# A graph convolution on one core: eight groups of every twenty routed on chip instead of seven, with a new order of work

## The chip, the cores and the metric

The kernel runs on one core of a Trainium2 chip. The metric is the device time in microseconds of one execution. The kernel before took 2231.55 us (median of three runs, 2224.62 to 2231.94).

## The reference

```
h   = x @ W_in2f                                     # 6250 nodes x 128
Wij = (ssp(f_ij @ W_filt1 + b_filt1) @ W_filt2 + b_filt2) * weight[:, None]   # 200000 edges
agg = segment_sum(h[dst] * Wij, src, 6250)           # a sum per node over its edges
out = ssp(agg @ W_out1 + b_out1) @ W_out2 + b_out2   # ssp(v) = softplus(v) - log 2
y   = layernorm(x + out)
```

The edges are sorted by `dst`, so the rows `h[dst]` of neighbouring edges lie close together. `src`, the index of the sum, is in random order. Everything is float32; `f_ij` has 20 columns.

## The kernel before

**Tiling.** 200000 edges are 391 groups of 512 (four tiles of 128). Twenty groups make a *unit*; there are 19 full units and a rest of eleven groups (380 to 390). A prologue forms `h`, splits it into three bf16 parts, writes it to HBM, and works out positions for the routed groups. An epilogue adds the partial sums and does the two output layers and the layer norm in 13 chunks.

**Every group** goes through the same front part. TensorE does the first filter layer for two groups at once (`first_layer`, L1773). ScalarE takes abs, exp and ln of it, VectorE finishes `hidden` (L1301). TensorE does the second layer (`second_layer`, a bias matmul at L1782 and the product at L1786). TensorE picks the rows `h[dst]` from a window of 128 rows with a one-hot (`gather`, L1811), ScalarE scales them by the edge weight (L874), and VectorE multiplies the two (`multiply`, L1327) into the message.

**How a message is summed** is one of two ways. A *plain* group builds an equality matrix `same` (VectorE L1280), TensorE sums repeated indices within a tile (`sum_repeated`, L1799), ScalarE copies the result out (`copy_total`, L857), VectorE makes the index (`mark_repeated` L1337, `make_index` L1346), and GpSimd issues four indirect DMAs, one for each tile, that add 128 rows of 512 B into one of four tables in HBM (`scatter`, L716). `total` has four buffers, and `copy_total` waits until the adds of the plain group that held its buffer have landed (`rows_landed`).

A *routed* group never leaves the chip. ScalarE and VectorE split its message into two float32r parts (`split_hi` L885, `split_lo` L1353). VectorE builds four one-hots of 128x896 (`route_one_hot`, L1365). TensorE multiplies them to sort the messages into seven slot tiles (`route`, four matmuls each, L1829). ScalarE keeps each in a ring of seven (`keep_slots`, L898). Then one slot tile for each of the seven newest groups gets a one-hot (`slot_one_hot`, L1382), TensorE sums the seven (`sum_slots`, 28 matmuls, L1848), and VectorE adds the two halves of the result to `acc_t` (`add_slice`, L1399). `route_hot` has one buffer and `unit_psum` two banks, used by `route` and `sum_slots` in turn: `route(m, 0)` and `route(m, 1)` wait for the two adds of the sums before them, and later ones wait for the ring copy two back.

**Order.** TensorE, ScalarE and VectorE each follow a list written out by hand for a unit (`unit(u)`), and another for the rest (`rest()`). GpSimd and SyncE go group by group. `m(n)` and `r(n)` count routed groups in the unit, `g(n)` groups, `pair(n)` pairs. `ROUTED_AT` says which groups of a unit are routed: seven of twenty, and three in the rest, 136 in all.

Of the kernel before, what the change touches and what calls it, by code (L numbers as in the profile page):

```python
# [60 lines left out]
META_HOTS, META_STEPS = 20, 49  # L61
# [15 lines left out]
assert BUCKETS * BUCKET == NODE_ROWS > NODES and RING == PER_UNIT == SLOT_TILES and UNIT % 4 == 0  # L77
# [200 lines left out]
def build(nc, t):  # L278
    with ExitStack() as ctx:
# [89 lines left out]
        local = at(39872, "local", [P, ROUTES * TILES], F32)  # L369
        src_r = at(42048, "src_r", [P, ROUTES * TILES], I32)  # L370
        rank = at(44224, "rank", [P, UNITS * PER_UNIT * TILES], F32)
        rank_part = at(46464, "rank_part", [P, ROUTES * TILES], F32)
        in_bucket = at(48640, "in_bucket", [P, BUCKETS, ROUTES * TILES], BF16)
        h_rest = at(63872, "h_rest", [P, 2, 4, DIM], F32)
        bias_tmp = at(67968, "bias_tmp", [P, 2, 3, DIM], F32)
        bias_hi = at(71040, "bias_hi", [P, 2, 3, DIM], BF16)
        base_all = at(72576, "base_all", [P, SLOTS], F32)
        spread_row = at(74208, "spread_row", [1, SLOTS], F32)
# [386 lines left out]
        def _(act):  # L765
# [135 lines left out]
            def unit(u):  # L901
                def g(n): return plus(u, n)
                def pair(n): return (u[0], u[1] // 2 + n)
                def m(n): return (u[0], u[1] // UNIT * PER_UNIT + n)
                def r(n): return (u[0], u[1] // UNIT * PER_UNIT + n)
                soften_ln(pair(2))
                keep_slots(m(0), 0)
                weigh_h_dst(g(3), plain)
                copy_total(g(0), plain)
                keep_slots(m(0), 1); keep_slots(m(0), 2)  # L910
                soften_abs(pair(3))
                keep_slots(m(0), 3); keep_slots(m(0), 4)
                soften_exp(pair(3))
                keep_slots(m(0), 5); keep_slots(m(0), 6)
                soften_ln(pair(3))
                weigh_h_dst(g(4), plain)
                split_hi(r(0))
                weigh_h_dst(g(5), plain)
                copy_total(g(1), plain)
                weigh_h_dst(g(6), plain)  # L920
                soften_abs(pair(4))
                keep_slots(m(1), 0)
                copy_total(g(3), plain)
                keep_slots(m(1), 1)
                soften_exp(pair(4))
                keep_slots(m(1), 2)
                soften_ln(pair(4))
                keep_slots(m(1), 3); keep_slots(m(1), 4); keep_slots(m(1), 5); keep_slots(m(1), 6)
                split_hi(r(1))
                columns(g(10), plain)  # L930
                soften_abs(pair(5))
                weigh_h_dst(g(7), plain)
                copy_total(g(4), plain)
                soften_exp(pair(5))
                weigh_h_dst(g(8), plain)
                soften_ln(pair(5))
                keep_slots(m(2), 0); keep_slots(m(2), 1); keep_slots(m(2), 2); keep_slots(m(2), 3)
                copy_total(g(6), plain)
                keep_slots(m(2), 4)
                weigh_h_dst(g(9), plain)  # L940
                keep_slots(m(2), 5)
                weigh_h_dst(g(10), plain)
                keep_slots(m(2), 6)
                split_hi(r(2))
                soften_abs(pair(6))
                soften_exp(pair(6))
                soften_ln(pair(6))
                copy_total(g(7), plain)
                keep_slots(m(3), 0)
                weigh_h_dst(g(11), plain)  # L950
                copy_total(g(9), plain)
                keep_slots(m(3), 1); keep_slots(m(3), 2); keep_slots(m(3), 3); keep_slots(m(3), 4)
                weigh_h_dst(g(12), plain)
                soften_abs(pair(7))
                keep_slots(m(3), 5); keep_slots(m(3), 6)
                soften_exp(pair(7))
                soften_ln(pair(7))
                weigh_h_dst(g(13), plain)
                split_hi(r(3))
                weigh_h_dst(g(14), plain)  # L960
                copy_total(g(10), plain)
                soften_abs(pair(8))
                keep_slots(m(4), 0)
                soften_exp(pair(8))
                weigh_h_dst(g(15), plain)
                keep_slots(m(4), 1); keep_slots(m(4), 2)
                soften_ln(pair(8))
                keep_slots(m(4), 3); keep_slots(m(4), 4); keep_slots(m(4), 5); keep_slots(m(4), 6)
                copy_total(g(12), plain)
                weigh_h_dst(g(16), plain)  # L970
                split_hi(r(4))
                soften_abs(pair(9))
                soften_exp(pair(9))
                weigh_h_dst(g(17), plain)
                keep_slots(m(5), 0)
                soften_ln(pair(9))
                copy_total(g(13), plain)
                keep_slots(m(5), 1); keep_slots(m(5), 2)
                columns(g(20), plain)
                weigh_h_dst(g(18), plain)  # L980
                keep_slots(m(5), 3); keep_slots(m(5), 4); keep_slots(m(5), 5)
                soften_abs(pair(10))
                keep_slots(m(5), 6)
                soften_exp(pair(10))
                soften_ln(pair(10))
                copy_total(g(15), plain)
                split_hi(r(5))
                weigh_h_dst(g(19), plain); weigh_h_dst(g(20), plain)
                soften_abs(pair(11))
                keep_slots(m(6), 0); keep_slots(m(6), 1)  # L990
                soften_exp(pair(11))
                keep_slots(m(6), 2); keep_slots(m(6), 3)
                soften_ln(pair(11))
                keep_slots(m(6), 4)
                weigh_h_dst(g(21), plain)
                keep_slots(m(6), 5); keep_slots(m(6), 6)
                copy_total(g(17), plain)
                split_hi(r(6))
                soften_abs(pair(12))
                weigh_h_dst(g(22), plain)  # L1000
                soften_exp(pair(12))
                copy_total(g(18), plain)

            def rest():
                weigh_h_dst((0, 383), plain)
                keep_slots((0, 133), 0)
                soften_ln((0, 192))
                keep_slots((0, 133), 1); keep_slots((0, 133), 2)
                copy_total((0, 380), plain)
                keep_slots((0, 133), 3)  # L1010
                soften_abs((0, 193))
                keep_slots((0, 133), 4); keep_slots((0, 133), 5); keep_slots((0, 133), 6)
                weigh_h_dst((0, 384), plain)
                soften_exp((0, 193))
                soften_ln((0, 193))
                copy_total((0, 381), plain)
                split_hi((0, 133))
                weigh_h_dst((0, 385), plain)
                soften_abs((0, 194))
                weigh_h_dst((0, 386), plain)  # L1020
                keep_slots((0, 134), 0)
                copy_total((0, 383), plain)
                keep_slots((0, 134), 1); keep_slots((0, 134), 2); keep_slots((0, 134), 3)
                keep_slots((0, 134), 4); keep_slots((0, 134), 5); keep_slots((0, 134), 6)
                split_hi((0, 134))
                soften_exp((0, 194))
                soften_ln((0, 194))
                weigh_h_dst((0, 387), plain)
                copy_total((0, 384), plain); copy_total((0, 386), plain)
                keep_slots((0, 135), 0); keep_slots((0, 135), 1); keep_slots((0, 135), 2)  # L1030
# [687 lines left out]
        def _(pe):  # L1718
# [135 lines left out]
            def unit(u):  # L1854
# [3 lines left out]
                def r(n): return (u[0], u[1] // UNIT * PER_UNIT + n)  # L1858
# [264 lines left out]
```

## Time and profile before

| | us |
|---|---|
| median of three runs | 2231.55 |
| lowest and highest run | 2224.62, 2231.94 |
| span of the profiled execution | 2225.5 |
| TensorE matmul busy, weight load busy | 2054.4 (92%), 1691.5 (76%) |
| VectorE busy | 1898.8 (85%) |
| ScalarE busy | 1594.9 (72%) |
| GpSimd busy | 1754.4 (79%) |

The profile gives no time of its own for the profiled execution besides its span, 2225.5 us; the three runs lie between 0.9 us below and 6.4 us above that. The busy shares are means over prologue, main part and epilogue. The main part is from about 105 to 2140 us.

### The profile page before, as it was taken

What the parts mean: (1) busy time and instruction counts of PE and PEld (TensorE: products, weight loads), DVE (VectorE), ACT (ScalarE), POOL (GpSimd) and SP (SyncE); (2) the same over time, 40 slices, a digit from 0 to 9 for tenths busy, and PEclk for the clock granted to TensorE, in tenths of its full rate; (3) what the DMA queues carried; (4) which work ended last, traced back from release to release, by engine and by line L of the source; (5) the groups of instructions that cost most, each with busy time, mean ns of one, the idle gap of its engine ahead of it and who ended that gap; (6) DMA issues with size and microseconds to landing.
All of it is one profiled execution on the core that took longest, in us unless ns stands there. A gap on an engine that the chain in (4) does not pass through costs nothing.

```text
span 2225.5 us, 54062 instructions
## 1 busy us (share of the span) xinstructions
PE 2054.4 (92%) x15953; PEld 1691.5 (76%) x15953; DVE 1898.8 (85%) x3919; ACT 1594.9 (72%) x3812; POOL 1754.4 (79%) x1078
## 2 busy tenths in 40 slices
PE   3589999999999999999999999999999999999946
PEld 2477878787887878887888788888878887877733
DVE  6578989898998988988999888988989988988837
ACT  0378777777777777877777777877777777877617
POOL 2058888888888888888888888888888888888874
PEclk9699999999999999999999999999999999999978
DMA  9556666665666565655666656656666665666495
GB/s 329 191 99 95 97 100 99 89 100 90 98 98 100 93 92 92 107 96 87 102 97 96 97 90 97 98 92 96 96 101 97 95 99 92 93 100 94 52 223 141
DMA packets 353785, 239.34 MB, mean 108 GB/s; under 512 B 86919, under 2 KB 332786, under 8 KB 353338
## 3 DMA queue, kind: packets, MB, share of 16 engines
q0 software_dynamic: 146736, 66.85, 32.2%
q1 hardware_dynamic: 196326, 152.61, 27.4%
q10 hardware_dynamic: 10476, 16.77, 2.0%
q8 instruction: 133, 2.18, 0.4%
q14 instruction: 114, 0.93, 0.1%
HBM read 147.25 MB, written 88.83 MB: 106 GB/s over the span
## 4 chain that ended last, share of the span: by engine, by line
DMA 33%; PE 30%; POOL 14%; issue 13%; DVE 5%; ACT 4%; POOLq 0%; ACTq 0%; DVEq 0%; SPq 0%
DMA table<-total,index 31%; POOL table L716 14%; PE unit_psum L1829 7%; PE unit_psum L1848 6%; PE both_psum L1786 6%; PE total_psum L1799 4%; PE pre_psum L1773 3%; PE both_psum L1811 2%; PE both_psum L1782 2%; DMA h_parts<-h_out 1%; ACT out_rows L1087 1%; ACT total L857 1%; DMA b_o<-in_b_o 1%; DVE scat_hot L1382 1%; DVE route_hot L1365 0%
## 5 line engine op out<-in xcount | busy, mean ns | idle before, releaser
L716 POOL DMA_INDIRECT table<-total,index x1019 | 1695.7, 1664 | 419.6 <-issue 252.5
L1829 PE MATMUL unit_psum<-moving,route_hot 128*128 128x258 f32 x3808 | 604.7, 298 | 5.5 <-ACT ring L898 3.2
L1829 PEld LDWEIGHTS unit_psum<-moving,route_hot 128*128 128x128 f32 x3808 | 497.9, 192 | 68.6 <-ACT ring L898 49.9
L898 ACT ACTIVATE ring<-unit_psum 128x258 fp32r<-128x258 f32 x952 | 354.1, 394 | 242.6 <-PE unit_psum L1829 225.5
L874 ACT ACTIVATE h_dst<-both_psum,cols 128x128 f32<-128x128 f32 x1564 | 446.3, 374 | 95.3 <-PE both_psum L1811 92.5
L1848 PE MATMUL unit_psum<-scat_hot,ring 64*128 64x448 f32 x3808 | 462.2, 380 | 8.1 <-DVE acc_t L1399 4.2
L1382 DVE TENSOR_SCALAR scat_hot<-node_iota,ring 128x448 fp32r<-128x448 uint16 x952 | 434.7, 476 | 6.8 <-ACT ring L898 4.7
L1786 PEld LDWEIGHTS both_psum<-w_f,hidden 128*128 128x128 f32 x3128 | 426.1, 197 | 11.8
L1786 PE MATMUL both_psum<-w_f,hidden 128*128 128x128 f32 x3128 | 423.9, 279 | 0.0
L1365 DVE TENSOR_SCALAR route_hot<-node_iota,cols 128x896 fp32r<-128x896 uint16 x544 | 378.4, 713 | 43.7 <-PE unit_psum L1829 42.9
L1848 PEld LDWEIGHTS unit_psum<-scat_hot,ring 64*128 64x128 f32 x3808 | 340.2, 186 | 87.5 <-ACT ring L898 30.3
L1799 PE MATMUL total_psum<-message,same 128*128 128x129 f32 x2040 | 284.7, 283 | 33.9 <-ACT total L857 33.1
L1799 PEld LDWEIGHTS total_psum<-message,same 128*128 128x128 f32 x2040 | 258.2, 197 | 56.8 <-issue 54.2
L1301 DVE SCALAR_TENSOR_TENSOR hidden<-pre_psum,soft 128x1024 f32<-128x1024 f32 x196 | 238.3, 1216 | 45.3 <-ACT soft L850 45.2
L857 ACT ACTIVATE total<-total_psum 128x516 f32<-128x516 f32 x255 | 154.7, 607 | 119.8 <-DMA table<-total,index 110.1
L1773 PE MATMUL pre_psum<-f_t,w_f 32*128 32x512 f32 x784 | 222.8, 644 | 7.0 <-issue 4.3
L838 ACT ACTIVATE soft<-pre_psum 128x1024 f32<-128x1024 f32 x196 | 201.8, 1030 | 30.4 <-PE pre_psum L1773 30.1
L1327 DVE TENSOR_TENSOR message<-both_psum,h_dst 128x512 f32<-128x512 f32 x255 | 174.2, 683 | 43.6 <-PE both_psum L1786 40.7
L844 ACT ACTIVATE soft<-soft 128x1024 f32<-128x1024 f32 x196 | 209.7, 1070 | 1.3
L850 ACT ACTIVATE soft<-soft 128x1024 f32<-128x1024 f32 x196 | 208.8, 1065 | 2.0
L1399 DVE TENSOR_TENSOR acc_t<-acc_t,unit_psum 128x448 f32<-128x448 f32 x284 | 166.8, 611 | 11.4 <-PE unit_psum L1848 10.8
L1811 PE MATMUL both_psum<-window,pick 128*128 128x128 bf16 x1564 | 158.1, 225 | 16.6 <-DVE pick L1291 10.0
(118 smaller groups left out, 1517.7 us busy)
## 6 DMA issues: line engine op xcount, KB each, us to landing
dst_b<-dst SPq DMA_DIRECT2D x391, 128.0 KB
src_b<-src SPq DMA_DIRECT2D x255, 128.0 KB
f_t<-in_f_t SPq DMA_DIRECT2D x100, 256.0 KB, 3.7
table<-total,index POOLq DMA_INDIRECT x1019
table<-zeros ACTq DMA_DIRECT2D x20, 640.0 KB, 10.1
window<-h_parts SPq DMA_DIRECT2D x391, 32.0 KB
parts<-table SPq DMA_DIRECT2D x48, 256.0 KB, 5.4
h_parts<-h_out SPq DMA_DIRECT2D x12, 384.0 KB, 2.9
```

Source lines behind the costliest of these rows:

```text
L716: pool.indirect_dma_start(tables[table], bass.IndirectOffsetOnAxis(index[:, i, k:k + 1], 0), total[:, i, k, 0:DIM], None, compute_op=ALU.a ...
L844: act.activation(soft[:, :, :], soft[:, :, :], ACT.Exp, scale=-1.0).then_inc(exp_done, 1)
L874: last = act.activation(h_dst[:, b, d], source, ACT.Copy, scale=cols[:, g[1] // HALF % 2, weight:weight + 1])
L898: act.activation(ring[:, r[1] % RING, k, :], unit_psum[:, k % 2, 0:MOVING], ACT.Copy).then_inc(ring_done, 1)
L1301: dve.scalar_tensor_tensor(hidden[:, first:first + 2, :], pre_psum[:, :, :], 0.0, soft[:, :, :], ALU.max, ALU.add).then_inc(hidden_done, 1)
L1365: hot = dve.tensor_scalar(route_hot[:, tile, :], node_iota[:, :], cols[:, half, column:column + 1], None, ALU.is_equal)
L1382: dve.tensor_scalar(scat_hot[:, r[1] % RING, :], node_iota[:, 0:BUCKET], ring[:, r[1] % RING, k, 2 * DIM:2 * DIM + 1].bitcast(F32), None, ...
L1773: last = pe.matmul(pre_psum[:, a, :], w_f1[row:row + BAND, :], f_t[row:row + BAND, quad[1] % FEEDS, :], start=True, stop=True)
L1786: last = pe.matmul(filter_psum[:, d], hidden[:, g[1] % QUAD, k * P:(k + 1) * P], w_f2[:, :], start=False, stop=(k == TILES - 1))
L1799: last = pe.matmul(total_psum[:, k // 2, d], same[:, b, k, :], message[:, b, k, :], start=True, stop=True)
L1829: last = pe.matmul(unit_psum[:, k % 2, 0:MOVING], route_hot[:, tile, k * P:(k + 1) * P], moving[:, tile, :], start=(tile == 0), stop=(tile ...
L1848: last = pe.matmul(unit_psum[:, strip, 0:BUCKET], ring[rows, r[1] % RING, slot_tile(m), part * DIM:(part + 1) * DIM], scat_hot[rows, r[1] ...
```

## The change

`ROUTED_AT` gets an eighth group in every unit, and the rest a fourth: 156 routed groups and 235 plain ones instead of 136 and 255. The arrays for the routed groups' positions grow with them (624 columns instead of 544). A memset in the prologue goes, and a wait for the column copy is written out ahead of the one-hots. The order lists of TensorE, ScalarE and VectorE are written anew, for the unit and for the rest; the ring of seven and the sums over seven groups stay.

```diff
-ROUTED_AT = (2, 5, 8, 11, 14, 16, 19)
-LAST_ROUTED = (382, 385, 387)
+ROUTED_AT = (1, 3, 6, 8, 11, 13, 16, 18)
+LAST_ROUTED = (381, 383, 386, 388)
 PER_UNIT = len(ROUTED_AT)
-FIRST_ROUTED = 3
+FIRST_ROUTED = 4
...
-META_HOTS, META_STEPS = 20, 49
+META_HOTS, META_STEPS = 20, 48
...
-        local = at(39872, "local", [P, ROUTES * TILES], F32)
+        local = at(40192, "local", [P, ROUTES * TILES], F32)
...
-                dve.memset(slots[:, :, 0, n:4 * TILES], 0.0).then_inc(meta_step, 1)
...
             def route_one_hot(r, tile):
...
                 if routes(plus(r, -1)) and tile == 0:
                     dve.wait_ge(route_mm_done, through_tile(plus(r, -1), SLOT_TILES - 1))
+                dve.wait_ge(cols_done, through_half(group_of(r)))
...
             def rest():
-                route((0, 133), 2); route((0, 133), 3); route((0, 133), 4)
-                first_layer((0, 193))
-                second_layer((0, 383))
+                sum_repeated((0, 379), plain)
+                route((0, 152), 2); route((0, 152), 3)
+                gather((0, 382))
+                second_layer((0, 381))
```

On **TensorE**, around the sum of slots. In the rows, `scat_hot,ring` is `sum_slots` (28 matmuls make one full sum), `moving,route_hot` is `route` (four matmuls for one slot tile), `window,pick` is `gather`, `f_t` the first layer, `bias_f` and `w_f,hidden` the second layer, `message,same` is `sum_repeated`. Before, in a unit of the main part:

```order
L1773 MATMUL pre_psum<-f_t,w_f 128x512 x2
L1848 MATMUL unit_psum<-scat_hot,ring 128x448 x24
L1799 MATMUL total_psum<-message,same 128x129 x4
L1848 MATMUL unit_psum<-scat_hot,ring 128x448 x4
L1811 MATMUL both_psum<-window,pick 128x128 x4
L1782 MATMUL both_psum<-bias_f,ones_bias 128x512
L1786 MATMUL both_psum<-w_f,hidden 128x128 x4
L1829 MATMUL unit_psum<-moving,route_hot 128x258 x4
L1799 MATMUL total_psum<-message,same 128x129 x4
L1829 MATMUL unit_psum<-moving,route_hot 128x258 x8
L1773 MATMUL pre_psum<-f_t,w_f 128x512 x2
```

Now, in the same part of the program:

```order
L1813 MATMUL pre_psum<-f_t,w_f 128x512 x2
L1822 MATMUL both_psum<-bias_f,ones_bias 128x512
L1826 MATMUL both_psum<-w_f,hidden 128x128 x4
L1888 MATMUL unit_psum<-scat_hot,ring 128x448 x28
L1851 MATMUL both_psum<-window,pick 128x128 x4
L1839 MATMUL total_psum<-message,same 128x129 x4
L1869 MATMUL unit_psum<-moving,route_hot 128x258 x4
L1822 MATMUL both_psum<-bias_f,ones_bias 128x512
L1826 MATMUL both_psum<-w_f,hidden 128x128 x4
L1869 MATMUL unit_psum<-moving,route_hot 128x258 x4
L1813 MATMUL pre_psum<-f_t,w_f 128x512 x2
L1869 MATMUL unit_psum<-moving,route_hot 128x258 x4
```

Before, four of a unit's seven sums of slots are cut by other work, and of its 49 `route` steps 40 stand in pairs. Now all eight sums stand whole, and of 56 `route` steps 34 stand alone.

On **VectorE**, from the first `route_one_hot` of a routed group (`route_hot`) to its two `add_slice` (`acc_t`). `scat_hot` is `slot_one_hot`, `moving` is `split_lo`, `pick` is `compare_dst`, `moved` is `mark_repeated`. Before, at the sixth routed group of a unit:

```order
L1365 TENSOR_SCALAR route_hot<-node_iota,cols 128x896 x3
L1327 TENSOR_TENSOR message<-both_psum,h_dst 128x4x128
L1382 TENSOR_SCALAR scat_hot<-node_iota,ring 128x448 x2
L1365 TENSOR_SCALAR route_hot<-node_iota,cols 128x896
L1291 TENSOR_SCALAR pick<-dst_b,cols 128x512
L1301 SCALAR_TENSOR_TENSOR hidden<-pre_psum,soft 128x1024
L1382 TENSOR_SCALAR scat_hot<-node_iota,ring 128x448
L1353 TENSOR_TENSOR moving<-message_r,moving 128x4x128
L1337 TENSOR_SCALAR moved<-total,order_twice,spare_row 128x4
L1399 TENSOR_TENSOR acc_t<-acc_t,unit_psum 128x448 x2
```

Now, at the seventh of a unit:

```order
L1390 TENSOR_SCALAR route_hot<-node_iota,cols 128x896 x2
L1407 TENSOR_SCALAR scat_hot<-node_iota,ring 128x448
L1390 TENSOR_SCALAR route_hot<-node_iota,cols 128x896
L1407 TENSOR_SCALAR scat_hot<-node_iota,ring 128x448
L1390 TENSOR_SCALAR route_hot<-node_iota,cols 128x896
L1377 TENSOR_TENSOR moving<-message_r,moving 128x4x128
L1424 TENSOR_TENSOR acc_t<-acc_t,unit_psum 128x448 x2
```

Other work (a message, a pick, a hidden, a mark) stood between the one-hots and the adds, and is now ahead of them or behind.

## Rows read from the trace of the kernel before

**Rows 1.** The page: its costliest group.
```profile
L716 POOL DMA_INDIRECT table<-total,index x1019 | 1695.7, 1664 | 419.6 <-issue 252.5
```

**Rows 2.** Groups of GpSimd and VectorE, 500 to 1500 us.
```profile
L716 POOL DMA_INDIRECT table<-total,index x507 | 846.2, 1669 | 154.7 <-issue 120.8 <-DMA table<-total,index 26.8 <-ACT total L857 4.0
L1382 DVE TENSOR_SCALAR scat_hot<-node_iota,ring 128x448 fp32r<-128x448 uint16 x478 | 218.5, 475 | 2.2 <-ACT ring L898 2.1
L1365 DVE TENSOR_SCALAR route_hot<-node_iota,cols 128x896 fp32r<-128x896 uint16 x272 | 190.0, 716 | 22.1 <-PE unit_psum L1829 22.0
```

**Rows 3.** The timeline of GpSimd: the first scatter and the last.
```profile
127.16 1.73 POOL L716 DMA_INDIRECT table<-total,index  x1 [104.75 <-DVE index L1346]
...
2136.21 1.54 POOL L716 DMA_INDIRECT table<-total,index  x1 [0.30 <-issue]
```

**Rows 4.** Stretches: PE, PEld, DVE, ACT, POOL busy; clock, DMA, GB/s.
```profile
500.00:1526.00 1026.00, 1002.35 (x7966) 834.01 (x7964) 912.89 (x1872) 782.91 (x1881) 867.38 (x521) 0.98 0.62 96
724.00:728.00 4.00, 4.00 (x21) 3.14 (x19) 4.00 (x9) 3.23 (x7) 3.39 (x3) 0.50 0.45 63
```

**Rows 5.** The timeline around 720 us.
```profile
721.68 0.60 ACT L857 ACTIVATE total<-total_psum 128x516 f32<-128x516 f32 x1 [5.79 <-DMA table<-total,index]
722.43 2.06 PE L1799 MATMUL total_psum<-message,same 128*128 128x129 f32 x8 [3.03 <-ACT total L857]
```

**Rows 6.** The timeline of PE: second layers; the outer two are the first and last.
```profile
109.25 0.61 PE L1782 MATMUL both_psum<-bias_f,ones_bias 96*128 96x512 bf16 x1
...
552.12 0.38 PE L1782 MATMUL both_psum<-bias_f,ones_bias 96*128 96x512 bf16 x1
...
650.43 0.38 PE L1782 MATMUL both_psum<-bias_f,ones_bias 96*128 96x512 bf16 x1
...
754.91 0.38 PE L1782 MATMUL both_psum<-bias_f,ones_bias 96*128 96x512 bf16 x1
...
2110.86 0.39 PE L1782 MATMUL both_psum<-bias_f,ones_bias 96*128 96x512 bf16 x1
```

**Rows 7.** The timeline of PE, back to back; last, a full sum of slots.
```profile
1050.22 0.40 PE L1811 MATMUL both_psum<-window,pick 128*128 128x128 bf16 x4
1050.55 0.68 PE L1848 MATMUL unit_psum<-scat_hot,ring 64*128 64x448 f32 x4
1051.15 1.13 PE L1773 MATMUL pre_psum<-f_t,w_f 32*128 32x512 f32 x4
...
1055.21 1.20 PE L1829 MATMUL unit_psum<-moving,route_hot 128*128 128x258 f32 x8
1056.25 1.06 PE L1799 MATMUL total_psum<-message,same 128*128 128x129 f32 x8
1057.06 0.73 PE L1829 MATMUL unit_psum<-moving,route_hot 128*128 128x258 f32 x4
1057.63 0.39 PE L1782 MATMUL both_psum<-bias_f,ones_bias 96*128 96x512 bf16 x1
...
1061.19 3.12 PE L1848 MATMUL unit_psum<-scat_hot,ring 64*128 64x448 f32 x28
1064.25 0.40 PE L1811 MATMUL both_psum<-window,pick 128*128 128x128 bf16 x4
```

**Rows 8.** The timeline of VectorE, one-hots of a routed group.
```profile
1158.47 0.67 DVE L1365 TENSOR_SCALAR route_hot<-node_iota,cols 128x896 fp32r<-128x896 uint16 x1
...
1161.37 0.67 DVE L1353 TENSOR_TENSOR moving<-message_r,moving 128x512 fp32r<-128x512 f32 x1
```

**Rows 9.** The timeline of the last sums of slots, and the loads behind them.
```profile
2124.69 2.74 PE L1848 MATMUL unit_psum<-scat_hot,ring 64*128 64x448 f32 x24 [1.72 <-DVE scat_hot L1382]
2129.11 2.56 PE L1848 MATMUL unit_psum<-scat_hot,ring 64*128 64x448 f32 x20 [1.68 <-DVE acc_t L1399]
...
2140.15 45.50 SPq L659 DMA_DIRECT2D parts<-table  x52
```

**Rows 10.** The timeline of VectorE in the prologue.
```profile
59.45 0.72 DVE L1214 TENSOR_TENSOR rank<-rank,rank_part 128x544 f32<-128x544 f32 x1
```

More of the change, by code:

```diff
@@ new lines, in unit @@
+                multiply(g(1), plain)
+                slot_one_hot(m(1), 3)
+                mark_repeated(g(0), plain)
+                route_one_hot(r(0), 0)
+                slot_one_hot(m(1), 4)
+                make_index(g(0), plain)
+                route_one_hot(r(0), 1); route_one_hot(r(0), 2)
+                multiply(g(2), plain)
+                route_one_hot(r(0), 3)
+                slot_one_hot(m(1), 5); slot_one_hot(m(1), 6)
+                split_lo(r(0))
+                slot_one_hot(m(2), 0)
@@ new lines, in unit @@
+                second_layer(g(1))
+                route(m(0), 5)
+                gather(g(3))
+                route(m(0), 6)
+                first_layer(pair(2))
+                second_layer(g(2))
+                sum_slots(m(1), 0); sum_slots(m(1), 1); sum_slots(m(1), 2); sum_slots(m(1), 3)
+                sum_slots(m(1), 4); sum_slots(m(1), 5); sum_slots(m(1), 6)
+                gather(g(4))
+                sum_repeated(g(2), plain)
+                route(m(1), 0)
+                second_layer(g(3))
@@ new lines, in unit @@
+                route(m(5), 1)
+                first_layer(pair(8))
+                route(m(5), 2)
+                second_layer(g(14))
+                route(m(5), 3)
+                gather(g(15))
+                route(m(5), 4)
+                second_layer(g(15))
+                route(m(5), 5)
+                sum_repeated(g(14), plain)
+                route(m(5), 6)
+                gather(g(16))
+                first_layer(pair(9))
+                sum_slots(m(6), 0); sum_slots(m(6), 1); sum_slots(m(6), 2); sum_slots(m(6), 3)
@@ L1941, in unit @@
+                route(m(6), 2)
+                gather(g(18))
+                route(m(6), 3); route(m(6), 4)
+                sum_repeated(g(17), plain)
+                route(m(6), 5)
+                gather(g(19))
+                route(m(6), 6)
                 first_layer(pair(10))
-                route(m(5), 5); route(m(5), 6)
+                sum_slots(m(7), 0); sum_slots(m(7), 1); sum_slots(m(7), 2); sum_slots(m(7), 3)
+                sum_slots(m(7), 4); sum_slots(m(7), 5); sum_slots(m(7), 6)
@@ L1951, in unit @@
+                gather(g(21))
+                route(m(7), 6)
                 first_layer(pair(11))
[L1952 removed]
+                sum_slots(m(8), 0); sum_slots(m(8), 1); sum_slots(m(8), 2); sum_slots(m(8), 3)
+                sum_slots(m(8), 4); sum_slots(m(8), 5); sum_slots(m(8), 6)
                 second_layer(g(20))
[L1954 to L1957 removed]
@@ new lines, in rest @@
+                gather((0, 386))
+                route((0, 153), 4); route((0, 153), 5)
+                second_layer((0, 385))
+                route((0, 153), 6)
+                sum_repeated((0, 384), plain)
+                sum_slots((0, 154), 0); sum_slots((0, 154), 1); sum_slots((0, 154), 2); sum_slots((0, 154), 3)
+                sum_slots((0, 154), 4); sum_slots((0, 154), 5); sum_slots((0, 154), 6)
+                gather((0, 387))
+                first_layer((0, 194))
+                route((0, 154), 0); route((0, 154), 1)
```

866 lines of the change are left out of this document (435 added, 431 removed).

## The prediction

> **What bounds the kernel now.** The page comes first. It shows TensorE at 92% and GpSimd at 79%, which points at TensorE. The row of the scatters says otherwise: 1019 of them have 1695.7 us of work and 419.6 us of idle time ahead of them, and 252.5 us of that waited for nothing [rows 1]. The groups of the steady part show why: 507 scatters in 1000 us have 846.2 us of work and 154.7 us of gaps, together the whole of it [rows 2]. A scatter takes 1.669 + 0.305 = 1.974 us, and the queue is never empty from the first scatter at 127.16 us to the last at 2136.21 us [rows 3]. A unit has 13 plain groups, so 52 scatters, 102.6 us.
>
> The starts of the second layers check this. From the first, 109.25, to the last, 2110.86, there are 390 groups in 2001.6 us, 102.65 us for a unit of 20 [rows 6]. GpSimd sets the pace.
>
> The same rows show how. Twenty groups take 98.3 us from 552.12 on and 104.5 us from 650.43 on [rows 6]. TensorE runs ahead for a unit or so, until ScalarE stands still for 5.79 us at a copy of `total`, whose buffer waits for its adds to land, and TensorE stands still for 3.03 us behind it [rows 5]. Then its granted clock is 0.50 for some microseconds, 1.2 of its 2.4 GHz [rows 4]. The stretch of 98.3 us is TensorE left to itself: in it the matmuls follow back to back, and I take it as what TensorE needs for a unit. So TensorE has 4.3 us of room in 102.6, not the 8% that the page suggests. VectorE is busy 912.9 of 1026 us [rows 4], 91.3 us a unit.
>
> **GpSimd.** A unit has 12 plain groups now: 48 x 1.974 = 94.8 us. It falls out of the lead by 7.9 us a unit. With it go the stalls of ScalarE and the stretches at 1.2 GHz behind them, as the plain groups are never more than two in a row and four buffers of `total` stand ahead. What is late next is TensorE.
>
> **TensorE** gets one routed group more. By starts in back-to-back stretches, two `route` steps together take 1.04 us, one alone 0.57, `sum_repeated` 0.81, a whole sum of slots 3.06 [rows 7].
> - `route`: before 20 pairs and 9 alone, 20.8 + 5.1 = 25.9 us; now 11 pairs and 34 alone, 11.4 + 19.4 = 30.8 us: +4.9.
> - `sum_slots`: one whole sum more: +3.1.
> - `sum_repeated`: one fewer: -0.8.
> - Cuts. Before, seven extra breaks stand in a unit's sums of slots. A piece of four matmuls takes 0.60 us against 3.06 / 7 = 0.44 within a whole sum, and the `gather` ahead of it 0.33 [rows 7] against some 0.20 ahead of a `route`: 0.3 for a break, -2.1. There are also fewer `gather` steps directly ahead of a first layer, and fewer second layers and repeated sums ahead of a `gather` or a sum; I estimate -1.5 for these.
>
> Together +3.6: TensorE needs 98.3 + 3.6 = 101.9 us. If the cuts are worth nothing, it is 105.5; if the single steps cost no more than paired ones, 101.9 - 25 x 0.05 = 100.7. I take 101.9, because breaks and singles are both read from rows of this trace.
>
> **VectorE** gets four `route_one_hot` of 716 ns, seven `slot_one_hot` of 475 [rows 2], a `split_lo` and two adds, less a `same`, a `moved` and an `index`: 2.9 + 3.3, and some 0.7 for the rest, +6.9 us. Busy then is 98.2 of 101.9 us. Records of neighbours overlap by some 0.08 us, so it isn't full, but its cover for a late step shrinks from 11 to 4 us of shown idle time. ScalarE gets a split and seven ring copies less one `copy_total`, about 3 us, and has over 20 to spare. The added wait for the columns is for something long done: 0. SyncE issues 20 loads of `src_b` fewer, on no path.
>
> **Prologue.** VectorE's 27 steps on 544 columns, 0.72 us each [rows 10], go to 624 columns, with 14 one-hots before them. At 15% more of their column part that is an estimated +3.3 us, all on the path, because the node features wait behind them. The removed memset saves under 0.1.
>
> **The end.** From the last second layer to the loads of the tables it is 2140.15 - 2110.86 = 29.3 us now [rows 6, 9]; the last scatters set it. With GpSimd on time it will be TensorE: behind the last second layer come seven `route` steps, two repeated sums and a whole sum, about 13 us with their handovers, and then the seven left-over batches, 28 steps in all. A batch of six takes 4.42 us [rows 9], 1.8 more than its 6 x 0.44, since the next batch waits for one-hots and adds. So 28 x 0.44 + 7 x 1.8 + 1.1 for the last add = 26 us. Together 39.3 us, 10 more than now. The first seven sums in turn lack those 28 steps, -12 us, and filling the pipe costs an estimated 3: -9.
>
> **Sum**, against the span of 2225.5 us: first second layer at 109.25 + 3.3 = 112.6; 19.5 x 101.9 = 1987.1; -9; the end 39.3; and 85.3 us from the loads to the end as now: 2215.3 us, 10.2 less. The median of the runs lies 6 us above the span, so 2231.55 - 10.2 = 2221.3 us. A change of 0.5%, 11 us, is about the least that can be told here.
>
> **Rivals.**
> - *Handovers on VectorE* (slower). From the last `route` of a group to the first of the next, TensorE has a first layer (1.06), a sum (3.06) and a second layer (1.03), 5.15 us, at the tightest places of the new order. In that time VectorE must wait for the last `route`, make four one-hots of 896 columns and two small ones, then `split_lo` and one add: the first five are 1161.37 - 1158.47 = 2.90 us [rows 8], plus 0.36 + 0.60 + 0.53 = 4.4 us, and two semaphores. Half a microsecond is left. If VectorE is late because a `hidden` (1.1 us) still runs, TensorE waits. Each 0.1 us at each of 156 routed groups is 15.6 us; from 0.14 us the change is slower by over 0.5%. With 0.25 us it is 39 us, 2260. For it: VectorE at 98 of 102 us, and an order with no stall of GpSimd in which to catch up. Against it: the new order clears other work from between one-hots and adds, and in the 98.3 us stretch such handovers cost nothing visible.
> - *TensorE packs closer* (faster). The steps stand further apart from what they wait for, since most `route` steps are alone, so small waits that the 98.3 us still hold go: 100.5 us a unit, 27 us less, 2194. Against it: that stretch has few such waits.
> - *GpSimd stays the bound* (far faster). If TensorE had the room, a unit would fall to 94.8 us: 19.5 x 7.9 = 153 us less, and about 2079 us. For it: weight loads are busy only 834 of 1026 us [rows 4]. Against it: the starts of the matmuls leave no room, as above. The Trainium skill (Perfetto Trace Analysis, "Identifying the Most-Contended Engine") says that matmul busy time is not a good measure of distance to roofline and that the busy share of weight loads is a better one. By that rule TensorE would be 19% from full and this rival would hold; the back-to-back starts of the trace speak against it for products with 258 and 448 columns.
> - *The change doesn't do what it says* (TensorE waits at GpSimd as before): 48 scatters in bursts could still fill the buffers. Two plain groups in a row are 15.8 us of scatters in about 10 us, made up by the next routed one; the buffers reach four groups, 20 us. About no change; I give it little.
>
> **How the numbers follow.** The forecast, TensorE as the bound at 101 to 102.6 us a unit, has 0.47, and its own range is 2205 to 2236 us. TensorE closer has 0.17, GpSimd still the bound 0.04, late handovers 0.27, bursts 0.05. A little under half of the forecast's own range lies below 2220.4 us, so faster is 0.21 + 0.17 + 0.04 = 0.42; slower is nearly all of the late handovers, 0.25; the rest, 0.33, is within 0.5%. The range for 8 in 10 reaches into both neighbours: 2192 to 2262 us.
>
> **What would show it.** Right: gaps ahead of scatters much over 0.30 us, and ScalarE no longer waiting for landed adds at L857's copy; units of second layers alike at about 102 us; granted clock near 1.00 throughout; the loads of the tables some 39 us behind the last second layer. Wrong: idle time of TensorE at its first two `route` steps (waits for one-hots or adds of VectorE) of over a microsecond a unit, or scatters still back to back.

## The result, and the profile after

The changed kernel takes 2276.86 us (median of four runs, 2270.05 to 2283.82) against 2228.09 us for the kernel before (four runs, 2223.24 to 2231.94). The ratio is 1.0205, with a 95% interval of 1.0169 to 1.0242: slower, by about 2%. The forecast was 2221.3 us, and its range ended at 2262. The profiled execution after has a span of 2281.7 us and took 2283.82 us.

Split at the same points as in the prediction, the span shows where the time went. The column e5 is the best kernel of the experiments, explained below.

| us | before | forecast | after | e5 |
|---|---|---|---|---|
| start to first second layer | 109.3 | 112.6 | 114.3 | 114.6 |
| 19 units (380 groups) | 1934.8 | 1927.1 | 1980.2 | 1932.9 |
| second layers of the rest | 66.8 | 51.0 | 45.8 | 45.7 |
| last second layer to table loads | 29.3 | 39.3 | 55.3 | 42.6 |
| table loads to end | 85.3 | 85.3 | 86.1 | 85.4 |
| span | 2225.5 | 2215.3 | 2281.7 | 2221.2 |

The forecast's 1927.1 is 19 x 101.9 - 9, and its 51.0 is half a unit. The rows of three of the cuts after: the first second layer, that of group 380 and the last. They answer to [rows 6] (timeline of TensorE: start, duration, engine, line, operation), and the same three rows of e5 with its loads of the tables stand behind them:

```profile
114.29 0.61 PE L1822 MATMUL both_psum<-bias_f,ones_bias 96*128 96x512 bf16 x1
...
2094.46 0.39 PE L1822 MATMUL both_psum<-bias_f,ones_bias 96*128 96x512 bf16 x1
...
2140.29 0.38 PE L1822 MATMUL both_psum<-bias_f,ones_bias 96*128 96x512 bf16 x1
```

```profile
114.62 0.61 PE L1839 MATMUL both_psum<-bias_f,ones_bias 96*128 96x512 bf16 x1
...
2047.53 0.39 PE L1839 MATMUL both_psum<-bias_f,ones_bias 96*128 96x512 bf16 x1
...
2093.21 0.38 PE L1839 MATMUL both_psum<-bias_f,ones_bias 96*128 96x512 bf16 x1
...
2135.77 46.22 SPq L659 DMA_DIRECT2D parts<-table  x52
```

Two parts miss the forecast by much: the units by 53.1 us, the end by 16.0. First the units. The page after, costliest groups (busy time, mean ns of one, then idle time ahead of them and what ended most of it), answers to [rows 1]:

```profile
L716 POOL DMA_INDIRECT table<-total,index x939 | 1580.0, 1683 | 566.0 <-issue 307.5
...
L1304 DVE TENSOR_TENSOR same<-src_b,cols 128x512 f32<-128x512 uint16 x235 | 158.7, 682 | 58.9 <-issue 55.3
```

GpSimd did leave the lead, as forecast: a scatter costs what it did, but there are 80 fewer of them and 146 us more idle time. The second row is new. VectorE stands idle for 58.9 us ahead of `same`, a step ahead of which it had 1.5 us of idle time in the kernel before. The windows answer to [rows 4]:

```profile
500.00:1526.00 1026.00, 1015.44 (x8315) 858.95 (x8313) 952.77 (x1953) 799.26 (x1931) 793.59 (x472) 1.00 0.59 90
```

TensorE is busy 99% here, and VectorE 952.8 of 1026 us, 39.9 more than before. The list of waits names what little TensorE lacks (waiting engine, line and releaser; us in total, times, longest):

```profile
PE unit_psum L1888 <- DVE scat_hot L1407: 24.9, 43, 1.2
...
PEld unit_psum L1888 <- DVE scat_hot L1407: 45.1, 64, 1.5
...
DVE same L1304 <- issue: 55.3, 21, 4.0
```

21 waits of VectorE at `same` are about one in a unit, and TensorE (PE, and PEld for its weight loads) waits for the one-hots of a sum of slots. "issue" says that the profile shows no releaser; a load from SyncE's queue is one that it can miss, so the timeline has to show it. One unit around 1133 us, SyncE's queue first, then VectorE, then TensorE:

```profile
1127.85 0.33 SPq L587 DMA_DIRECT2D window<-h_parts  x1
1129.96 0.33 SPq L554 DMA_DIRECT2D dst_b<-dst  x1
1132.67 0.33 SPq L587 DMA_DIRECT2D window<-h_parts  x1
1133.19 0.33 SPq L560 DMA_DIRECT2D src_b<-src  x1
...
1133.09 1.27 DVE L1304 TENSOR_TENSOR same<-src_b,cols 128x512 f32<-128x512 uint16 x2
1137.48 0.69 DVE L1304 TENSOR_TENSOR same<-src_b,cols 128x512 f32<-128x512 uint16 x1 [3.11 <-issue]
1138.09 0.45 DVE L1407 TENSOR_SCALAR scat_hot<-node_iota,ring 128x448 fp32r<-128x448 uint16 x1
1138.45 1.28 DVE L1390 TENSOR_SCALAR route_hot<-node_iota,cols 128x896 fp32r<-128x896 uint16 x2
...
1132.10 0.40 PE L1851 MATMUL both_psum<-window,pick 128*128 128x128 bf16 x4
...
1136.64 2.62 PE L1888 MATMUL unit_psum<-scat_hot,ring 64*128 64x448 f32 x20
1140.14 0.68 PE L1888 MATMUL unit_psum<-scat_hot,ring 64*128 64x448 f32 x4 [0.88 <-DVE scat_hot L1407]
1141.10 0.67 PE L1888 MATMUL unit_psum<-scat_hot,ring 64*128 64x448 f32 x4 [0.28 <-DVE scat_hot L1407]
1141.70 0.39 PE L1822 MATMUL both_psum<-bias_f,ones_bias 96*128 96x512 bf16 x1
```

The new order of VectorE has three `compare_src` in a row in the middle of the one-hots for the seventh sum of slots, for groups 19, 20 and 22 (counted on into the next unit). The third needs the load of `src_b` for group 22. SyncE issues that load at 1133.19, behind the load of the same group's window. That one waits until TensorE has done the `gather` four groups back, at 1132.10, since `window` has four buffers. The trace has no landing for this load, but VectorE goes on at 1137.48, 4.3 us after its issue, and three one-hots of the sum come behind it. The sum takes 1141.70 - 1136.64 = 5.06 us instead of 3.06 [rows 7].

In some units more is lost. The same place two units earlier, timeline of TensorE:

```profile
930.51 0.67 PE L1888 MATMUL unit_psum<-scat_hot,ring 64*128 64x448 f32 x4 [1.18 <-DVE scat_hot L1407]
931.46 0.95 PE L1888 MATMUL unit_psum<-scat_hot,ring 64*128 64x448 f32 x4 [0.28 <-DVE scat_hot L1407]
932.34 0.61 PE L1822 MATMUL both_psum<-bias_f,ones_bias 96*128 96x512 bf16 x1
932.74 1.92 PE L1826 MATMUL both_psum<-w_f,hidden 128*128 128x128 f32 x8
934.31 1.56 PE L1869 MATMUL unit_psum<-moving,route_hot 128*128 128x258 f32 x8
```

And the windows on both sides of it (columns as in [rows 4]; the clock is the third number from the end):

```profile
928.00:930.00 2.00, 0.67 (x4) 0.30 (x4) 2.00 (x5) 1.94 (x3) 1.70 (x2) 1.00 0.61 57
930.00:932.00 2.00, 1.21 (x8) 0.62 (x8) 2.00 (x5) 0.27 (x1) 1.70 (x2) 0.92 0.24 18
932.00:934.00 2.00, 2.00 (x11) 1.57 (x8) 1.93 (x5) 0.00 (x0) 1.42 (x1) 0.50 0.22 23
```

TensorE worked 1.88 of the 4 us from 928 on, and then its granted clock was 0.50, 1.2 GHz. The second layer takes 934.31 - 932.34 = 1.97 us instead of 1.03. So here the wait cost TensorE another 0.94 us on top of its own length. Of the 18 units behind the first, ten take 103.0 to 104.2 us between second layers and eight 104.4 to 106.9.

The end: TensorE's last batches, then the loads of the tables. They answer to [rows 9].

```profile
2166.02 5.25 PE L1888 MATMUL unit_psum<-scat_hot,ring 64*128 64x448 f32 x28 [3.86 <-DVE acc_t L1424]
2174.76 4.85 PE L1888 MATMUL unit_psum<-scat_hot,ring 64*128 64x448 f32 x24 [3.50 <-DVE acc_t L1424]
2182.74 4.10 PE L1888 MATMUL unit_psum<-scat_hot,ring 64*128 64x448 f32 x20 [3.13 <-DVE acc_t L1424]
2189.61 3.35 PE L1888 MATMUL unit_psum<-scat_hot,ring 64*128 64x448 f32 x16 [2.77 <-DVE acc_t L1424]
...
2195.63 30.88 SPq L659 DMA_DIRECT2D parts<-table  x35
```

VectorE's rows of the same stretch show where the 3.86 and 3.50 us come from:

```profile
2162.28 2.63 DVE L1407 TENSOR_SCALAR scat_hot<-node_iota,ring 128x448 fp32r<-128x448 uint16 x7 [1.29 <-PE unit_psum L1888]
2164.82 1.14 DVE L1424 TENSOR_TENSOR acc_t<-acc_t,unit_psum 128x448 f32<-128x448 f32 x2
2171.38 2.27 DVE L1407 TENSOR_SCALAR scat_hot<-node_iota,ring 128x448 fp32r<-128x448 uint16 x6 [5.42 <-PE unit_psum L1888]
2173.56 1.15 DVE L1424 TENSOR_TENSOR acc_t<-acc_t,unit_psum 128x448 f32<-128x448 f32 x2
```

`rest()` now puts all one-hots of the next batch ahead of the two adds of the last one, and the next batch waits for the adds. So 2.27 to 2.63 us of one-hots stand between two batches, in series with them. The batch of 24 matmuls (six groups) has a gap of 3.50 us where that of the kernel before with as many matmuls has 1.72 [rows 9], and it takes 4.85 us where the other takes 2.74, since the clock is at half in part of this stretch. From its start to the next it is 8.0 us (2182.74 - 2174.76), and 4.42 before [rows 9].

### The profile page after: what moved, and what is told of

It is laid out like the page before. It is cut to its first block and busy times, and to the rows that moved or that the text cites. A ratio compares the mean times of both kernels' runs of the same rounds, so it can differ in the third digit from the quotient of the medians.

```text
span 2281.7 us, 56428 instructions
## 1 busy us (share of the span) xinstructions
PE 2127.8 (93%) x16913; PEld 1779.5 (78%) x16913; DVE 2009.6 (88%) x4138; ACT 1653.9 (72%) x3972; POOL 1638.7 (72%) x998
## 5 line engine op out<-in xcount | busy, mean ns | idle before, releaser
L716 POOL DMA_INDIRECT table<-total,index x939 | 1580.0, 1683 | 566.0 <-issue 307.5
L1869 PE MATMUL unit_psum<-moving,route_hot 128*128 128x258 f32 x4368 | 738.8, 299 | 3.8 <-DVE acc_t L1424 3.5
L898 ACT ACTIVATE ring<-unit_psum 128x258 fp32r<-128x258 f32 x1092 | 423.1, 392 | 339.3 <-PE unit_psum L1869 323.5
L1869 PEld LDWEIGHTS unit_psum<-moving,route_hot 128*128 128x128 f32 x4368 | 579.1, 191 | 38.3 <-issue 19.0
L1888 PEld LDWEIGHTS unit_psum<-scat_hot,ring 64*128 64x128 f32 x4368 | 401.6, 188 | 198.3 <-ACT ring L898 87.1
L1888 PE MATMUL unit_psum<-scat_hot,ring 64*128 64x448 f32 x4368 | 513.1, 379 | 42.6 <-DVE scat_hot L1407 24.9
L1407 DVE TENSOR_SCALAR scat_hot<-node_iota,ring 128x448 fp32r<-128x448 uint16 x1092 | 504.2, 480 | 22.0 <-PE unit_psum L1888 19.8
L1390 DVE TENSOR_SCALAR route_hot<-node_iota,cols 128x896 fp32r<-128x896 uint16 x624 | 415.5, 696 | 15.7 <-PE unit_psum L1869 14.8
L1839 PE MATMUL total_psum<-message,same 128*128 128x129 f32 x1880 | 253.0, 277 | 1.2 <-DVE message L1351 1.1
L1304 DVE TENSOR_TENSOR same<-src_b,cols 128x512 f32<-128x512 uint16 x235 | 158.7, 682 | 58.9 <-issue 55.3
```

What stands on the lines that cost most here:

```text
L716: pool.indirect_dma_start(tables[table], bass.IndirectOffsetOnAxis(index[:, i, k:k + 1], 0), total[:, i, k, 0:DIM], None, compute_op=ALU.a ...
L898: act.activation(ring[:, r[1] % RING, k, :], unit_psum[:, k % 2, 0:MOVING], ACT.Copy).then_inc(ring_done, 1)
L1390: hot = dve.tensor_scalar(route_hot[:, tile, :], node_iota[:, :], cols[:, half, column:column + 1], None, ALU.is_equal)
L1407: dve.tensor_scalar(scat_hot[:, r[1] % RING, :], node_iota[:, 0:BUCKET], ring[:, r[1] % RING, k, 2 * DIM:2 * DIM + 1].bitcast(F32), None, ...
L1839: last = pe.matmul(total_psum[:, k // 2, d], same[:, b, k, :], message[:, b, k, :], start=True, stop=True)
L1869: last = pe.matmul(unit_psum[:, k % 2, 0:MOVING], route_hot[:, tile, k * P:(k + 1) * P], moving[:, tile, :], start=(tile == 0), stop=(tile ...
```

## The experiments

The kernel after was timed only in the result above. The kernel before was timed anew beside each set of experiments: its median was 2231.34 us beside e1 to e4, 2230.85 beside x1, x3, e5 and e6, and 2225.52 beside b1. Ratios are to the median of the same set. A difference in us between two sets, such as "less than after", is uncertain by some 3 us.

In the expectations, S is the theory of the load of `src_b`, T that of the order at the end, P the statement that GpSimd set the pace before and TensorE does after. H is the rival that VectorE as a whole is too full for the new order.

**e1: the third comparison later.** In VectorE's order alone, it stands behind a comparison for group 21:

```diff
-                compare_src(g(19), plain); compare_src(g(20), plain); compare_src(g(22), plain)
+                compare_src(g(19), plain); compare_src(g(20), plain)
...
                 compare_dst(g(21))
+                compare_src(g(22), plain)
```

> The changed kernel with one VectorE step moved: the compare of src for group 22 of a unit (compare_src(g(22))) stands eight steps later, behind compare_dst(g(21)). Theory S (late load): at its old place VectorE stands still about 3 us a unit for a src_b load that SyncE issues behind a window load, the last one-hots of the seventh sum of slots come late, and TensorE loses 2 to 5 us a unit, part of it at the lower clock. Then the stall goes, units of second layers fall from a mean of 104.7 to 102 to 102.7 us, and the time falls by 38 to 52 us, to 2225 to 2240 us. Rival H (VectorE is simply too full for the eighth routed group, as the prediction's handover rival has it): the place of one compare matters little, under 10 us, 2267 us or more.

Measured: 2238.47 us (2235.72 to 2240.05), ratio to before 1.0033 (1.0021 to 1.0046); span 2236.7. That is 38 us less than after. The 19 units take 1937.7 us, 42.5 less, and units behind the first 102.0 to 102.8. The end stays at 54.5 us. No instruction of VectorE was taken away, so H falls: VectorE does all its work, and a unit takes 102.5 us on average instead of 104.7.

**e2: the load earlier.** SyncE only:

```diff
-                load_window(g)
                 if plain(g[1]) and (not isinstance(g[0], int) or g[1] >= QUAD):
                     load_src(g, plain)
+                load_window(g)
```

> The changed kernel with SyncE's order alone changed: in each group the load of src_b is issued ahead of the load of the window, not behind it. VectorE's order stays. Theory S: the load for group 22 no longer waits for the gather of group 18, it is issued some 2.5 us earlier, and most of VectorE's 3.1 us goes: 25 to 50 us less, 2227 to 2252 us, unless the loads of windows, now behind a wait for an earlier compare, come late for gathers. Rival H: no change within 8 us.

Measured: 2234.27 us (2232.43 to 2236.54), ratio 1.002 (1.0006 to 1.0033); 43 us less than after. The timeline at the place that was shown above, SyncE's queue, then VectorE, then TensorE:

```profile
1108.22 0.33 SPq L560 DMA_DIRECT2D src_b<-src  x1
1110.42 0.33 SPq L587 DMA_DIRECT2D window<-h_parts  x1
...
1110.81 1.88 DVE L1304 TENSOR_TENSOR same<-src_b,cols 128x512 f32<-128x512 uint16 x3
...
1114.39 3.12 PE L1888 MATMUL unit_psum<-scat_hot,ring 64*128 64x448 f32 x28
1117.45 0.39 PE L1822 MATMUL both_psum<-bias_f,ones_bias 96*128 96x512 bf16 x1
```

The load goes out 2.2 us ahead of the window's instead of 0.5 behind it. The three comparisons run without a break, and the whole sum takes 3.06 us again. VectorE's order is untouched here, so the cause is the load's place behind another load that waits. A unit behind the first takes 102.3 us on average.

**e3: the end alone.** In `rest()`, the adds of a left-over batch stand ahead of the one-hots of the next. At one place the adds are those of the last full sum, at six those of a left-over batch. One of the six:

```diff
-                slot_one_hot((0, 161), 0); slot_one_hot((0, 161), 1); slot_one_hot((0, 161), 2)
-                slot_one_hot((0, 161), 3); slot_one_hot((0, 161), 4); slot_one_hot((0, 161), 5)
                 add_slice((0, 160), 0); add_slice((0, 160), 1)
+                slot_one_hot((0, 161), 0)
...
+                slot_one_hot((0, 161), 5)
```

> The changed kernel with the end of VectorE's rest() alone in another order: the two adds of each left-over batch of slots stand ahead of the one-hots of the next batch, not behind them. Theory T (one-hots ahead of adds): TensorE waits 3.9, 3.5, 3.1 and 2.8 us ahead of the last four batches, and its clock falls with it; with the adds first the waits fall to about 1.7 us, the batches from 8.7, 8.0, 6.9 us to 6.3, 4.4, 4.0, and the time by 9 to 14 us, 2263 to 2268 us. Rival: TensorE needs adds and one-hots of VectorE anyway, all of them, so the order does little: under 4 us.

Measured: 2262.49 us (2261.09 to 2266.85), ratio 1.014 (1.0109 to 1.0172), 14 us less than after, at the edge of what T allowed. From the last second layer to the loads it is 42.6 us instead of 55.3. T holds, and the units keep their loss (1976.6 us).

**e4: e1 and e3 together.**

> Both: the compare for group 22 eight steps later and the adds of left-over batches first. Theory S and T together: 47 to 66 us less than the changed kernel, 2211 to 2230 us, about the kernel before or up to 0.8% faster; the forecast's own 101.9 us a unit then holds within 0.6. Rival H: over 2255 us.

Measured: 2226.92 us (2224.03 to 2228.7), ratio 0.9984 (0.9969 to 0.9999), 50 us less than after. The two effects add up: 38 + 14 = 52.

**x1: the kernel before with cheap scatters.** Each scatter adds only the lower 64 of its 128 rows, so the upper 64 rows of every plain tile are left out of the sums:

```diff
-                    pool.indirect_dma_start(tables[table], bass.IndirectOffsetOnAxis(index[:, i, k:k + 1], 0),
-                                            total[:, i, k, 0:DIM], None, compute_op=ALU.add
+                    pool.indirect_dma_start(tables[table], bass.IndirectOffsetOnAxis(index[0:64, i, k:k + 1], 0),
+                                            total[0:64, i, k, 0:DIM], None, compute_op=ALU.add
```

> The kernel before with each scatter of 64 rows instead of 128: the upper 64 rows of every plain tile are left out of the sums. All waits, semaphores, and the number of scatters stay. Theory P (GpSimd sets the pace of the kernel before, and TensorE needs 98.3 us a unit when left alone): units of second layers fall from 102.65 to 98 to 99 us throughout, no wait of ScalarE for landed adds, and the time by 75 to 100 us, to about 2135 to 2155 us. Rival: the 98.3 us stretches are the easy half of a cycle that TensorE's own waits make, and the mean stays over 101 us: 2200 us or more.

Measured: 2138.41 us (2137.6 to 2140.2), ratio 0.9593 (0.9577 to 0.9609), 92 us less. Every unit behind the second takes 98.0 us. The windows from 500 to 1500 us and the group of the scatters in that stretch:

```profile
500.00:1500.00 1000.00, 1000.00 (x8119) 832.50 (x8119) 918.19 (x1910) 796.78 (x1920) 809.26 (x531) 1.00 0.49 84
```

```profile
L716 POOL DMA_INDIRECT table<-total,index x531 | 810.6, 1527 | 191.0 <-issue 173.6 <-DMA table<-total,index 15.3 <-DVE index L1346 1.2
```

A scatter's work falls from 1.669 us [rows 2] to 1.527 only, not to half. That is enough: 52 x (1.527 + 0.30) = 95 us a unit lies below the 98 us that TensorE needs, and TensorE is then busy all the time, at clock 1.00. The step of the prediction that took 98.3 us as TensorE's own need for a unit [rows 6] is confirmed within 0.3 us. The idle time of ScalarE that landing adds ended at its copy of `total`, 110.1 us in the kernel before, is 2.1 us here. The run halves the scattered bytes along with GpSimd's work, so it doesn't tell GpSimd's own time from that of its DMAs. That they are hard to part shows in [rows 2] too: of the 154.7 us ahead of 507 scatters, 26.8 were ended by adds that landed, and by estimate, without these a scatter would have 1.669 + 0.252 us and a unit 99.9 us instead of 102.6. So "GpSimd sets the pace" means its scatters together with the landing of their adds; the share of each is open.

**x3: e4 with the same cheap scatters**, and the same rows left out.

> The changed kernel with both mended places (compare for group 22 later, adds of left-over batches first) and each scatter of 64 rows instead of 128; the upper 64 rows of every plain tile are left out of the sums. Theory P: with eight routed groups TensorE is the bound, so lighter scatters change little: 0 to 8 us less than with both mended places alone, 2219 to 2227 us. Rival (bursts of scatters still hold it): 20 us less or more.

Measured: 2217.66 us (2215.91 to 2218.61), ratio to before 0.9945 (0.9929 to 0.9961). It is 9.3 us less than e4 (8.7 by the ratios, since e4 belongs to another set), a little more than P allowed, where the kernel before gained 92. A unit takes 102.0 us, and TensorE has no idle time from 500 to 1500 us:

```profile
500.00:1500.00 1000.00, 1000.00 (x8277) 855.20 (x8273) 933.82 (x1945) 796.35 (x1917) 754.10 (x472) 1.00 0.45 77
```

So x1 and x3 together measure what the change costs TensorE: 102.0 - 98.0 = 4.0 us a unit, or 1929.4 - 1854.4 = 75.0 us in 19 units. With scatters this cheap the change would lose all of that. At their real price nothing shows of it, because GpSimd held a unit at 102.5 us before.

**e5: e2 and e3 together.**

> The changed kernel with SyncE's load of src_b ahead of the load of the window, and the adds of left-over batches first. If the two effects add up as the single runs measured them (43 and 14 us less), 2220 to 2224 us, 0.3 to 0.5% faster than the kernel before. If they overlap at the end, 2226 us or more.

Measured: 2221.77 us (2219.52 to 2223.34), ratio 0.9964 (0.995 to 0.9978): faster than the kernel before, though by 0.4% only. Units behind the first take 102.0 to 102.6 us, the first 94.2. The windows, and the timeline of TensorE in the last batches:

```profile
500.00:1500.00 1000.00, 1000.00 (x8267) 853.70 (x8266) 949.76 (x1942) 795.10 (x1916) 786.29 (x471) 1.00 0.57 92
```

```profile
2116.22 4.79 PE L1905 MATMUL unit_psum<-scat_hot,ring 64*128 64x448 f32 x28 [1.70 <-DVE scat_hot L1407]
2122.71 2.71 PE L1905 MATMUL unit_psum<-scat_hot,ring 64*128 64x448 f32 x24 [1.70 <-DVE scat_hot L1407]
2127.12 2.30 PE L1905 MATMUL unit_psum<-scat_hot,ring 64*128 64x448 f32 x20 [1.70 <-DVE scat_hot L1407]
2131.12 1.89 PE L1905 MATMUL unit_psum<-scat_hot,ring 64*128 64x448 f32 x16 [1.70 <-DVE scat_hot L1407]
```

TensorE has no idle time in 1000 us. At the end the handover is 1.70 us, as in the kernel before [rows 9], and the batch of 24 matmuls costs 2127.12 - 2122.71 = 4.41 us.

**e6: e1, e2 and e3 together.**

> All three edits: src_b loaded ahead of the window, the compare for group 22 eight steps later, adds of left-over batches first. Theory S says that either of the first two takes the whole stall away, so both together bring nothing more: within 4 us of the run with the load first and the adds first, 2220 to 2226 us. If each took away a part, 2215 us or less.

Measured: 2225.97 us (2223.24 to 2228.21), ratio 0.9979 (0.9969 to 0.999). It brings nothing more than e5, as S says. It even takes 4.2 us more, just outside the 4 us expected. Ten of its twelve runs lie above all five of e5 (2219.52 to 2223.34), the median of e1 lies 4.2 us above that of e2, and in the profiled executions the 19 units of e6 take 1935.5 us against 1932.9. So the later place of the comparison seems to have a small price of its own, and e2's edit is the better one. The profiled executions don't show the 4 us as a whole (spans of 2220.5 and 2221.2, but that of e6 is one of its two fastest and that of e5 its slowest), and the reason is open.

**b1: the kernel before with the load of `src_b` first**, the edit of e2.

> The kernel before with one edit: SyncE issues the load of src_b ahead of the load of the window, as in e2. Theory S (the load of src_b, held behind the window's load on SyncE, ends a wait only where VectorE asks for it late in the unit and TensorE sets the pace): in the kernel before GpSimd's scatters set the pace at 102.7 us a unit, with VectorE's comparisons ahead of them, so this edit moves nothing: 2224 to 2238 us, ratio 0.997 to 1.003. Rival (the order of these two loads cost the kernel before something as well, so that what e2 won is no fault of the change): about 1 to 2 us on each of 19 units, 2192 to 2212 us.

Measured: 2224.9 us (2218.88 to 2230.8) against 2225.52, ratio 0.9996 (0.9982 to 1.001). Nothing moves. The order of the two loads was harmless until the change put a comparison close behind the load. What e2 wins is a loss that the change brought.

## Why the prediction was wrong

**What bounded the kernel before: right.** GpSimd set the pace, 102.5 us for a unit behind the first, and TensorE needed 98.3; x1 measured 98.0.

**TensorE's work: right, a little small.** The prediction added 3.6 us a unit, for 101.9 us. x3 against x1 shows 4.0, and 102.0 us. Most of the 0.4 is a miscount: the prediction credits seven breaks in a unit's sums of slots, but they stand in 13 pieces for seven sums, which is six breaks, 1.8 us and not 2.1. The credit of 9 us for the first sums is near: the first unit of e5 takes 94.2 us against 102.15 for the others, 8.0 less.

**Where the gain lies: in the traces, not where it was put.** The forecast had the units gain 7.7 us, and the rest with the end 5.8 (90.3 us together, 96.1 before). In e5 the 19 units gain 1.9 us: behind the first a unit falls from 102.5 to 102.15, 6.5 us in 18, but the first takes 94.2 us instead of 89.6, since GpSimd didn't hold it before either (90.4 in x1). The rest and the end go from 96.1 to 88.3 us together. With cheap scatters they take 88.7 in the old order (x1: 62.3 + 26.4) and 88.0 in the new one (x3: 45.5 + 42.5). So GpSimd's lag cost the kernel before at least 7.4 us there; at least, because in x1 too the loads of the tables start 2.3 us behind the last scatter and 4.9 us behind VectorE's last add. The change takes this lag away: 1.9 + 7.8 - 5.4 of prologue = 4.3 us of span, from 2225.5 to 2221.2. The large moves of the two rows in the table (21 us less, 13 more) are mostly sums of slots that now stand behind the last second layer; x3 against x1 shows the same (16.8 less, 16.1 more). The split is that of one pair of executions, and not a typical one: the medians differ by 9.1 us, and where the other 4.8 lie no trace here shows.

**SyncE: the step that failed.** The prediction said "SyncE issues 20 loads of `src_b` fewer, on no path". It counted SyncE's instructions and did not look at when each load's consumer comes in the new order, so the term stood at nothing. The wait at `same` was 1.5 us in all before, and so had no row among those that the argument rested on. The new order put `compare_src` for group 22 in a row with two others, where TensorE had just freed the window ahead of it (gather at 1132.10, loads at 1132.67 and 1133.19, the wait of 3.11 us ended at 1137.48). The cost, from the units of e5, is 1980.2 - 1932.9 = 47.3 us, 2.5 us for each of 19 units: 2.0 us of a stretched sum and now and then a stretch at half clock behind it. Either end of the dependence removes it (e1, e2), and both together bring no more (e6).

**The end: the second step that failed.** The prediction forecast 39.3 us and got 55.3. It took the handover between batches from [rows 9] (1.8 us more than the matmuls) although the change writes this order anew. There the adds of a batch now stand behind the next batch's one-hots. e3 puts them back and gets 42.6 us; 12.7 us of the miss are this order. The other 3.3 us are the term's own error: the prediction counted 0.44 us for each of the 28 steps of four matmuls, which is their time at full clock. In e5 the batches of two, one and seven take 3.6, 2.8 and 6.5 us from start to start instead of 2.7, 2.2 and 4.9, together 3.1 more. The granted clock was 0.50 from 2112 to 2116 us and 0.51 from 2116 to 2120; the batches of six and five, at full clock, take 4.4 and 4.0 us, as forecast.

**Prologue: right.** After takes 5.0 us more up to the first second layer, against 3.3. The steps on 624 columns take 0.81 us instead of 0.72 [rows 10], 27 x 0.09 = 2.4 us of it. All steps on these columns, from `rank_part` to `edge_cols`, go from 31.7 to 35.2 us, 3.5 more, which is the forecast's term. Another 1.1 us stand ahead of them: VectorE's cast of the indices, which waits for their load, starts at 20.97 us instead of 19.82.

**From span to median.** The forecast put the median 6 us above the span, since that of the three runs was. The profiled executions of the later kernels took some 2 us more than their spans (2283.82 and 2281.7), and the medians of after and e5 lie 4.8 us below and 0.6 us above the span. So the median of e5, 2221.77, is so near the forecast of 2221.3 us partly by chance. Measured alike, against the kernel before in its own set, e5 is 9.1 us faster (2230.85 to 2221.77), and the forecast had 10.2. By spans it is 5.9 us above the forecast's 2215.3: prologue 2.0, units 5.8, rest -5.3, end 3.3, and 0.1 behind it.

**The rivals.** Late handovers on VectorE were to give 2260 us, near what came, but by another mechanism. That one needed VectorE too full at 98 of 102 us. In e5 VectorE is busy 949.76 of 1000 us and TensorE never waits in that stretch. What made VectorE late was a transfer. GpSimd as the bound, and 94.8 us a unit, fell: with cheaper scatters a unit still takes 102.0 us (x3). Weight loads are busy 83% in x1 and 85% in e5 while TensorE has no idle time, and cheaper scatters gain e4 only 0.4%. The rule of the Trainium skill (Perfetto Trace Analysis, "Identifying the Most-Contended Engine"), that the busy share of weight loads tells better than that of matmuls how far TensorE is from full, does not hold for this kernel. The bursts of GpSimd cost little: adds that had not landed held ScalarE for 19.0 us in all in after, and for 110.1 in the kernel before.

## What to carry to other kernels

Where a change writes an order anew, go through every step whose operand comes by a transfer and ask when that transfer is issued, what is ahead of it in its queue and what that waits for. A wait of near zero in the old trace is no evidence for the new order. Put a load that depends on little ahead of one that waits, and between two uses of one buffer put the steps that free it first. Moving work off the engine that sets the pace puts it on another one. Here that one had only 4% of room, and the moved work nearly filled it. Measure its own need first, by making the work of the first engine cheaper.

## What was unexpected of the hardware

Half the rows of an indirect scatter save GpSimd little: 1.527 us for 64 rows against 1.669 for 128, with about 0.30 us between two issues in both. In this kernel the price hangs on the instruction more than on its rows.

A stretch of short gaps of TensorE, none longer than 1.2 us, was followed by a stretch at half clock (928 to 932 us busy 1.88 of 4 us; then 0.50 for 2 us), and at the end of after the mean clock from 2166 to 2196 us was 0.56, with TensorE busy 17.55 of 30 us. The same batches of e5 ran at 0.51 from 2116 to 2120 us, and at full clock from 2120 to 2136, with TensorE busy only 7.91 of 16 us. The gaps are 2.8 to 3.9 us long in after and 1.7 us in e5:

```profile
2116.00:2120.00 4.00, 3.78 (x20) 3.68 (x22) 2.28 (x7) 0.00 (x0) 2.92 (x2) 0.51 1.14 314
2120.00:2136.00 16.00, 7.91 (x70) 6.50 (x68) 10.05 (x23) 0.00 (x0) 1.96 (x2) 1.00 0.12 14
```

The busy share tells little here, since the same matmuls are busy longer at half clock: from 2116 to 2136 us e5 is busy 11.7 of 20 us, 58%, as after is from 2166 to 2196 us, but at a mean clock of 0.90 instead of 0.56. Whether a property of the gaps decides, and which, is left open.
